# A second block table in two parts, and block and expert numbers loaded 18 and 21 at a time

## The reference

```python
x = x + xattn(layernorm(x), ctx, pos, pos, Wq, Wkv, Wout, bout)   # 32 heads of 8, axial rope, softmax
x = x + ffn(layernorm(x), Wg, W1, W2, W3)

def ffn(x, Wg, W1, W2, W3):                                       # 8 experts, hidden size 176
    scores = einsum('btd,ed->bte', x, Wg)
    topk_s, topk_i = top_k(scores, 2)
    probs = softmax(topk_s)
    onehot = topk_i[..., None] == arange(E)
    w = einsum('btk,btke->bte', probs, onehot)
    for e in range(E):
        h = silu(einsum('btd,hd->bth', x, W1[e])) * einsum('btd,hd->bth', x, W2[e])
        y = y + w[..., e:e+1] * einsum('bth,dh->btd', h, W3[e])
    return y
```

## Time and profile before

| | us |
|---|---|
| median of 3 runs (529.56 to 529.92) | 529.66 |
| the profiled execution | 529.24 |
| its span, first to last instruction | 527.3 |
| PE busy | 474.1 (90%) |
| DVE busy | 405.5 (77%) |
| POOL busy | 366.0 (69%) |
| ACT busy | 351.6 (67%) |

### The profile page before, as it was taken

How to read it: one execution, slowest core, us unless ns; L and a number is a source line. 1 busy time by engine, 2 the same in 40 slices (tenths; PEclk the granted TensorE clock), 3 DMA queues, 4 the chain that set the end, 5 groups by cost and what they waited for, 6 DMA issues and landing times.

```text
span 527.3 us, 21533 instructions
## 1 busy us (share of the span) xinstructions
PE 474.1 (90%) x7701; PEld 365.8 (69%) x7701; DVE 405.5 (77%) x1199; ACT 351.6 (67%) x929; POOL 366.0 (69%) x634
## 2 busy tenths in 40 slices
PE   3676899999999999999999999889899999899890
PEld 2563566676676766767666665559799999889780
DVE  7376689899898999999989898767655556776672
ACT  3473677877778777777777777667466666566550
POOL 4442758888888888888888887356666557675471
PEclk9787999999999999999999999899899999999895
DMA  6920101121121212212111110143654446877844
GB/s 192 235 71 7 30 20 54 40 74 43 60 66 49 94 52 70 65 48 67 40 61 56 50 35 25 44 120 96 195 158 132 127 127 202 251 236 240 303 146 159
DMA packets 43225, 54.55 MB, mean 103 GB/s; under 512 B 6727, under 2 KB 36849, under 8 KB 43122
## 3 DMA queue, kind: packets, MB, share of 16 engines
q1 hardware_dynamic: 36066, 35.79, 24.5%
q0 software_dynamic: 6480, 16.85, 8.9%
q10 hardware_dynamic: 576, 0.53, 0.3%
HBM read 29.60 MB, written 23.94 MB: 102 GB/s over the span
## 4 chain that ended last, share of the span: by engine, by line
PE 69%; DVE 12%; DMA 6%; issue 6%; SPq 2%; ACT 2%; POOL 2%; POOLq 0%; DVEq 0%; ACTq 0%
PE logit_banks L1551 9%; PE bank L1401 6%; PE logit_banks L1570 6%; PE logit_banks L1361 6%; PE logit_banks L1342 5%; PE bank L1388 5%; PE qkv_banks L1310 5%; PE logit_banks L1369 5%; PE bank L1394 4%; PE qkv_banks L1321 3%; DVE negmax L757 3%; PE qkv_banks L1301 3%; DMA y_in<-result_rows 3%; PE bank L1331 3%; PE bank L1539 2%
## 5 line engine op out<-in xcount | busy, mean ns | idle before, releaser
L691 POOL DMA_INDIRECT result_rows<-blocks_io,blk_dest x71 | 72.5, 1021 | 53.3 <-ACT blocks_io L1245 23.8
L657 POOL DMA_INDIRECT routed_rows<-xs,slots x64 | 65.7, 1026 | 16.7 <-issue 16.7
L757 DVE TENSOR_REDUCE negmax<-logit_banks 128x16 f32<-128x1024 f32 x64 | 75.0, 1212 | 2.3 <-PE logit_banks L1342 2.3
L1137 ACT ACTIVATE late<-logit_banks 128x1024 f32<-128x1024 f32 x64 | 62.0, 1021 | 14.4 <-PE logit_banks L1369 14.4
L664 POOL TENSOR_TENSOR ropes<-rope_a,ropes 128x512 f32<-128x512 f32 x32 | 41.2, 1288 | 29.5 <-DVE ropes L744 29.5
L1022 DVE TENSOR_TENSOR gated<-xn,logit_banks 128x176 f32<-128x176 f32 x71 | 23.8, 335 | 46.8 <-ACT xn L1251 45.8
L764 DVE RECIPROCAL rden<-bank 128x256 f32<-128x256 f32 x32 | 55.8, 1745 | 0.8 <-PE bank L1394 0.8
L648 POOL TENSOR_TENSOR mid<-mid,mask 128x512 f32<-128x512 f32 x44 | 44.7, 1035 | 11.8 <-ACT mid L1118 11.7
L1551 PE MATMUL logit_banks<-w_hi,x_hi 128*128 x142 | 47.0, 331 | 0.0
L1551 PE MATMUL logit_banks<-w_hi,x_lo 128*128 x142 | 46.4, 327 | 0.0
L1251 ACT ACTIVATE xn<-logit_banks 128x176 f32<-128x176 f32 x71 | 22.5, 316 | 35.7 <-PE logit_banks L1551 35.7
(11 more groups left out here) (219 smaller groups left out, 1378.8 us busy)
## 6 DMA issues: line engine op xcount, KB each, us to landing
blocks_io<-routed_rows SPq DMA_DIRECT2D x71, 129.0 KB, 2.4
y_in<-result_rows SPq DMA_DIRECT2D x16, 512.0 KB, 4.6
x_sb<-in_x_dram SPq DMA_DIRECT2D x32, 128.0 KB, 2.1
out_dram<-o_sb SPq DMA_DIRECT2D x16, 256.0 KB, 3.8
ctx_sb<-in_ctx_dram SPq DMA_DIRECT2D x32, 64.0 KB, 2.3
blocks_io<-in_L_ffn_W_dram SPq DMA_DIRECT2D x4, 512.0 KB, 6.8
mid<-mT SPq DMA_DIRECT2D x128, 4.0 KB
routed_rows<-pad_row SPq DMA_DIRECT2D x11, 129.0 KB, 2.9
```

The source lines that it names most:

```text
L657: nc.gpsimd.indirect_dma_start(routed[:, :], bass.IndirectOffsetOnAxis(ap=slots[:, t.slot(TR), k:k + 1], axis=0), xs[:, t.slot(TR), k, :], ...
L691: nc.gpsimd.indirect_dma_start(results[:, :], bass.IndirectOffsetOnAxis(ap=blk_dest[:, b.slot(RB):b.slot(RB) + 1], axis=0), y_sb[:, b.slot ...
L757: V.tensor_reduce(negmax[:, t.par, 16 * half:16 * half + 16], ps_s[:, 1024 * half:1024 * half + 1024].rearrange("p (h k) -> p h k", k=N), ...
L1137: S.activation(pT[:, 1024 * half:1024 * half + 1024], ps_s[:, 1024 * half:1024 * half + 1024], ACT.Exp, scale=SCALE).then_inc(exp_done, 1)
```

## The change

The second table is worked out twice by the same steps: once from the counts up to tile 28 (five groups) for blocks 17 to 48 (`MID` is 49), in the last two turns of DVE's attention pipeline and around the first two block splits, and once from all counts for blocks 49 to 70, in DVE's turns 14 to 17. SP copies the first of them behind block 7's load and the second behind block 27's. The padding DMAs of SP move from behind block 11's load to behind block 15's. Row numbers are loaded at blocks 0, 17, 35 and 53 (17, then 18 at a time), expert numbers at 0 (17), and during blocks 16, 34 and 52, 21 at a time from numbers 14, 32 and 50, into one set of registers.

```diff
-    T1, NG = GROUPS[0], len(GROUPS)
-    FULL = 2 * T1 - E + 1
+    T1, T2, NG = GROUPS[0], GROUPS[-2], len(GROUPS)
+    FULL, MID = 2 * T1 - E + 1, 2 * T2 - E + 1
...
-            row_starts, row_counts = chunks(RB)
-            row_regs = [sp.alloc_register(f"row{n}") for n in range(max(row_counts))]
+            row_starts = [0, FULL, 2 * FULL + 1, 3 * FULL + 2, NBLK]
+            row_regs = [sp.alloc_register(f"row{n}") for n in range(FULL + 1)]
...
                 if c == FULL:
-                    sp.wait_ge(rest_in, 32)
                     sp.wait_ge(pad_in, 16 * E)
...
                 if c in row_starts:
-                    load_rows(c, row_counts[row_starts.index(c)])
+                    if c == FULL:
+                        sp.wait_ge(mid_in, 32)
+                    if c == row_starts[2]:
+                        sp.wait_ge(rest_in, 32)
+                    load_rows(c, row_starts[row_starts.index(c) + 1] - c)
                 load_block(Turn(0, c, RB))
-                if c == RB + 3:
+                if c == RB - 1:
+                    sp.wait_ge(mid_done, 2)
+                    sp.dma_start(row_i[0:1, FULL:MID], rest_i[FULL:MID, 0:1]).then_inc(mid_in, 16)
+                    sp.dma_start(exp_i[0:1, FULL:MID], rest_i[FULL:MID, 1:2]).then_inc(mid_in, 16)
+                if c == FULL - 2:
                     for e, rows in enumerate(load_counts(sp, 0)):
                         pad_expert(sp, e, rows)
-                if c == FULL - 3:
+                if c == JOIN + 20:
                     sp.wait_ge(rest_done, 2)
-                    sp.dma_start(row_i[0:1, FULL:NBLK], rest_i[FULL:NBLK, 0:1]).then_inc(rest_in, 16)
-                    sp.dma_start(exp_i[0:1, FULL:NBLK], rest_i[FULL:NBLK, 1:2]).then_inc(rest_in, 16)
+                    sp.dma_start(row_i[0:1, MID:NBLK], rest_i[MID:NBLK, 0:1]).then_inc(rest_in, 16)
+                    sp.dma_start(exp_i[0:1, MID:NBLK], rest_i[MID:NBLK, 1:2]).then_inc(rest_in, 16)
...
                 full_blocks(t.c - T1 - 3)
+                if t.c >= T2 + 2:
+                    rest_blocks(t.c - T2 - 2, NG - 1, mid_done)
...
-            def rest_blocks(step):
+            def rest_blocks(step, ng, done):
...
-                rest_blocks(b.c - JOIN)
+                if b.c >= 2 * JOIN:
+                    rest_blocks(b.c - 2 * JOIN, NG, rest_done)
...
             scores(tile(T - 2))
+            rest_blocks(2, NG - 1, mid_done)
             split_xbT(Turn(0, 0, RB))
+            rest_blocks(3, NG - 1, mid_done)
             split_xbT(Turn(0, 1, RB))
...
-            exp_starts, exp_counts = chunks(4)
-            ahead = [[pe.alloc_register(f"expert{k}_{n}") for n in range(max(exp_counts))] for k in range(2)]
+            exp_starts = [FULL, 2 * FULL + 1, 3 * FULL + 2]
+            ahead = [pe.alloc_register(f"expert{n}") for n in range(FULL + 4)]
...
-                k = exp_starts.index(first)
-                if first == 0:
-                    pe.wait_ge(full_in, 32)
-                if first == FULL:
-                    pe.wait_ge(rest_in, 32)
-                regs = ahead[k % 2][:exp_counts[k]]
-                pe.load(regs, exp_i[0:1, first:first + exp_counts[k]])
+                count = min(FULL + 4, (FULL if first == 0 else NBLK) - first)
+                pe.wait_ge(*{0: (full_in, 32), FULL - 3: (mid_in, 32)}.get(first, (rest_in, 32)))
+                pe.load(ahead[:count], exp_i[0:1, first:first + count])
...
                 if b.c + 1 in exp_starts:
-                    load_experts(b.c + 1)
+                    load_experts(b.c - 2)
```

More of the change, by code:

```diff
@@ L326, in xattn_ffn_kernel @@
         gap_done, lean_done = sem("gap_done"), sem("lean_done")
-        full_in, rest_in = sem("full_in"), sem("rest_in")
+        full_in, mid_in, rest_in, mid_done = (sem(s) for s in ("full_in", "mid_in", "rest_in", "mid_done"))
         wg_done, wg_sb = sem("wg_done"), sem("wg_sb")
@@ L407, in blocks @@
                 body(do, Turn(0, c, RB))
-        def chunks(step):
-            starts = list(range(0, FULL - step // 2, step)) + list(range(FULL, NBLK, step))
-            return starts, [end - start for start, end in zip(starts, starts[1:] + [NBLK])]
         def group_of(v):
@@ L980, in full_blocks @@
                     V.tensor_scalar(full_i[:, 1:2], full_exp[:], float(E - 1), None, ALU.min).then_inc(full_done, 1)
-            def rest_blocks(step):
+            def rest_blocks(step, ng, done):
                 flat = "p g e -> p (g e)"
+                n = ng * E
                 if step == 0:
-                    whole(ups[:].rearrange(flat), cnts[:].rearrange(flat), UP)
+                    whole(ups[:, 0:ng].rearrange(flat), cnts[:, 0:ng].rearrange(flat), UP)
                     V.tensor_copy(prior[:, 0], full_cnt[:])
-                    tab(V.tensor_copy(prior[:, 1:NG], ups[:, 0:NG - 1]))
+                    tab(V.tensor_copy(prior[:, 1:ng], ups[:, 0:ng - 1]))
@@ L989, in rest_blocks @@
                 if step == 1:
[L990 to L994, removed]
@@ L995, in rest_blocks @@
-                    tab(V.tensor_tensor(seg_skip[:], seg_from[:, 1:NG * E + 1], seg_from[:, 0:NG * E], ALU.subtract))
+                    V.scalar_tensor_tensor(seg_from[:, 0:n], prior[:, 0:ng].rearrange(flat), float(P),
+                                           region_g[:, 0:ng].rearrange(flat), ALU.mult, ALU.add)
+                    V.memset(seg_from[:, n:n + 1], float(E * RC))
+                    tab(V.tensor_tensor(seg_cnt[:, 0:n], ups[:, 0:ng].rearrange(flat), prior[:, 0:ng].rearrange(flat),
+                                        ALU.subtract))
@@ L996, in rest_blocks @@
+                    tab(V.tensor_tensor_scan(seg_end[:, 0:n], ones_g[:, 0:n], seg_cnt[:, 0:n], float(FULL),
+                                             ALU.mult, ALU.add))
+                    tab(V.tensor_tensor(seg_skip[:, 0:n], seg_from[:, 1:n + 1], seg_from[:, 0:n], ALU.subtract))
                 if step == 2:
-                    tab(V.scalar_tensor_tensor(seg_skip[:], seg_cnt[:], -float(P), seg_skip[:], ALU.mult, ALU.add))
+                    tab(V.scalar_tensor_tensor(seg_skip[:, 0:n], seg_cnt[:, 0:n], -float(P), seg_skip[:, 0:n],
+                                               ALU.mult, ALU.add))
@@ L1001, in rest_blocks @@
                 if step == 3:
-                    tab(V.tensor_reduce(rest_row[:], seg_jump[:], AX_X, ALU.add))
+                    tab(V.tensor_reduce(rest_row[:], seg_jump[:, 0:n], AX_X, ALU.add))
                     tab(V.scalar_tensor_tensor(rest_row[:], jcol[:], float(P), rest_row[:], ALU.mult, ALU.add))
-                    V.tensor_tensor(rest_i[:, 0:1], rest_row[:], rest_base[:], ALU.add).then_inc(rest_done, 1)
-                    V.tensor_reduce(rest_exp[:], seg_past[:], AX_X, ALU.add)
@@ L1006, in rest_blocks @@
-                    tab(V.tensor_reduce(seg_over[:], seg_past[:].rearrange("p (g e) -> p g e", e=E)[:, :, E - 1], AX_X,
-                                        ALU.add))
+                    if ng == NG:
+                        dve.wait_ge(mid_in, 32)
+                    V.tensor_tensor(rest_i[:, 0:1], rest_row[:], rest_base[:], ALU.add).then_inc(done, 1)
+                    V.tensor_reduce(rest_exp[:], seg_past[:, 0:n], AX_X, ALU.add)
+                    tab(V.tensor_reduce(seg_over[:], seg_past[:, 0:n].rearrange("p (g e) -> p g e", e=E)[:, :, E - 1],
+                                        AX_X, ALU.add))
@@ L1510, in body @@
                     transpose_weights(range(6, 8))
-            exp_starts, exp_counts = chunks(4)
-            ahead = [[pe.alloc_register(f"expert{k}_{n}") for n in range(max(exp_counts))] for k in range(2)]
+            exp_starts = [FULL, 2 * FULL + 1, 3 * FULL + 2]
+            ahead = [pe.alloc_register(f"expert{n}") for n in range(FULL + 4)]
             experts = {}
             def load_experts(first):
-                k = exp_starts.index(first)
-                if first == 0:
-                    pe.wait_ge(full_in, 32)
-                if first == FULL:
-                    pe.wait_ge(rest_in, 32)
-                regs = ahead[k % 2][:exp_counts[k]]
-                pe.load(regs, exp_i[0:1, first:first + exp_counts[k]])
-                for n, reg in enumerate(regs):
+                count = min(FULL + 4, (FULL if first == 0 else NBLK) - first)
+                pe.wait_ge(*{0: (full_in, 32), FULL - 3: (mid_in, 32)}.get(first, (rest_in, 32)))
+                pe.load(ahead[:count], exp_i[0:1, first:first + count])
+                for n, reg in enumerate(ahead[:count]):
                     experts[first + n] = pe.snap(reg, min_val=0, max_val=E - 1)
```

6 lines of the change are left out of this document (3 added, 3 removed).

## The result

| | before | after |
|---|---|---|
| median of 4 runs on one chip, us | 529.79 (529.56 to 529.94) | 540.95 (538.87 to 544.39) |
| ratio to before | | 1.0217 [1.0159, 1.0275] |
| span of the profiled execution, us | 527.3 | 542.5 |
| PE busy, us | 474.1 | 479.5 |

The change costs 11.2 us. The forecast was 5.4 slower, 535.0; the direction holds, and of the cost less than half was foreseen. The ratios leave out runs over 1.5% above the fastest of their kernel (one each of e2_pe_fours, e4_aligned and e8_before_pads13), which the ranges show.

The account below looks back on a forecast made before the run. PE, 69% of the chain, was taken to bound the kernel, losing time to padding and register loads. Terms -3.9 - 9.3 + 13.8 + 3.3 + 1.2 + 0.3 = +5.4 gave 535.0 us, range 522 to 541.

Parts of the forecast that it names:

- Prices: Register loads: starts on multiples of four are read four at a time (0.28 a four), others at 0.235 us a number.
- the first 17: First loads of 17 numbers from 0, on PE and SP: +1.2 us in all.
- the three small loads ahead of 17: PE's loads ahead of number 17: 0.34 us each, hidden below the cover of PE's queue, costing nothing.
- The rival of cheap numbers: PE's three long loads: a number costs little however many are read, +4.7 us, total 522.5; chance 0.22.
- that of pairs: Loads from 14 and 50: even starts are read in pairs, three loads cost 9.0 us, total 530.3; chance 0.26.
- that of number by number everywhere: All register loads: numbers read singly whatever the start, 5.0 us for 32 as well, total 543.9; chance 0.08.
- Block 12's wait: Pads moved behind block 15's load: block 12's load no longer waits, -2.2 idle and -1.7 half clock, -3.9 us.
- the forecast's 9.3 for small loads: Fourteen PE loads from number 17 on removed: twelve at 0.38, one 1.12, one 1.98 plus 1.65 half clock; -9.3 us.
- Block 17: Block 17's load waits for pads and SP's 18 row numbers: PE stands 2.2, half clock 1.1, +3.3 us.
- the last one of the change part by part: SP's table copies and 18-row loads at 35 and 53: eight buffers of lead, nothing, or up to 2 us in the tail.
- a stall of 4.8 for each long load: PE's loads of 21 from 14 and 50: 4.8 us idle each plus 1.7 half clock; all three loads +13.8.

Follow-up runs that it names:

- e2_pe_fours: Changed kernel with PE's expert numbers loaded four at a time from 17, 21, ... as before; 535.91 us, ratio 1.0114.
- e4_aligned: Changed kernel with every long register load on PE and SP begun on a multiple of four, sizes about 20; 529.24 us, ratio 1.0000.
- e8_before_pads13: Kernel before with SP's four pad DMAs behind block 13's load instead of block 11's; 526.43 us, ratio 0.9980.
- e7_before_aligned: Kernel before with the second table stored three places further, so every four and eight begins on a multiple of four; 522.00 us, ratio 0.9872.
- e6_best: Changed kernel with small loads of fours and eights, all begun on multiples of four, and pads behind block 13's load; 518.83 us, ratio 0.9804.
- e1_prices: Kernel before with 13 more register loads of expert numbers at the end of PE's program, their numbers unused; 530.41 us in one run.
- e1b_prices: Kernel before with 13 more register loads at the end of PE's program, each followed by a matmul using its last number; 540.01 us in one run.
- e9_rows53_early: Changed kernel with SP's 18 row numbers from 53 loaded behind block 36's load into registers of their own; 541.80 us, ratio 1.0218.

## Why the prediction was wrong

**Prices: right.** 5.09 for 14 and 50 (5.0 forecast), 1.74 for 32 (1.7), 4.03 for SP's 18 from 17 (3.7), 1.54 for the first 17 (1.4 without the start). The start of a run decides, as the rows of before suggested, and e7_before_aligned and e6_best show the other side of it. Two readings of those rows were wrong without harm: the load of five from 12 took 0.79, so not all three small loads ahead of 17 last 0.34, below the cover, and the four from 0 cost 0.13 a number and not 0.09. The rival of cheap numbers and that of pairs were refuted by rows, that of number by number everywhere by the load from 32, though its time, 543.9, lay nearer to the result. The Trainium skill ("Runtime: NRT & Kernel Launch", section "Instruction fetch mechanics") has about 200 ns a register even in bulk, on a page that speaks of loads from HBM; the tables here lie in SBUF. These runs are near that figure for unaligned starts (0.24) and not for aligned ones (0.08 in four or eight).

**Gains: right, in part by luck.** Block 12's wait gave 3.67 of 3.9, the small loads of h18 to h50 and h55 to h70 gave 9.7, where the forecast had 8.6 there. But of the forecast's 9.3 for small loads, 3.6 came from one long one, the 2.59 from 65 with the half clock behind it. The same load lasted 1.69, 2.03 and 1.14 in e1_prices, e1b_prices and e8_before_pads13, and the stage was 1.9 to 3.2 shorter there, so part of this gain belongs to the one profile of before that both were read from.

**Block 17: right in kind, too small in size.** The pads' issue ended near 382.1, within 1 us of the forecast's 377.5 once 3.8 of the first stage and 1.6 of t28 to h0 are added. But the last of them landed 5.4 after it began (chain of after: the pad's DMA, SP's numbers, block 17's DMA):

```profile
381.78 5.43 DMA routed_rows<-pad_row
387.23 4.03 SPq L517
...
392.05 1.95 DMA blocks_io<-routed_rows
```

The forecast took the median landing of 2.9 for it. PE stood 3.96 instead of the 2.2 forecast. Part came back at once, since the load from 14 behind it stood only 3.50 of its forecast 4.8.

**The step that failed** is the last one of the change part by part: SP's 18 rows at 35 and 53 "have eight buffers of lead: nothing, or up to 2 in the tail". At 35 that held. At 53 it cost 4.80 of idle PE, with a stretch of 6.7 at the 1.2 GHz level that begins just before PE goes on. h50 to h55 took 6.1 more than forecast, as much as the whole miss: PE's idle there was 4.80 and 2.33 where 4.8 was forecast, and 10 us ran at half clock (476.1 to 482.8 and 486.3 to 489.6) where 3.4 were forecast. The lead was counted for the blocks' loads, and block 53's load was late for nobody. The `y_in` loads on the same queue have no such lead: they already landed late in before (DVE waited 1.2 for two of them), and SP's queue held one of them back for 4.5. The instruction moved was looked at with the thing it serves, not with what stands behind it on its queue. Reading the same numbers 17 blocks earlier took that wait away and 3.9 off the stage (e9_rows53_early). The other 2.2 stay with PE's load from 50, which lasted 6.38 there instead of the 5.0 forecast. This is shown in the stage; the time of the whole kernel did not fall with it.

**Stalls are not a sum.** The forecast added a stall of 4.8 for each long load to the wait at block 17. Alone, PE stood 5.0 to 5.7 for such a load; right behind another wait only 3.50 and 2.33 in after. The error here was on the side of too much, and hid part of the other.

## What to carry to other kernels

Lay a table in SBUF so that every register load begins on a multiple of four numbers (16 bytes here): that was worth 1.3% [0.5, 2.0] to a kernel with 18 small loads on PE and 9 on SP. The two groupings by about 20 gained nothing: no change where they began on multiples of four, 2.2% slower where they did not. A register load, a count or a wait put into a queue that also issues transfers can be paid by whatever stands next in that queue with the least lead, as `y_in` did here, so list those by kind before calling a step free. And read an experiment by its stages, where two stalls lie close, since taking one away can let the next stand in full.

## What the runs showed of the hardware that was not expected

Two numbers from 18 or 20 took 0.54 and 0.55 us, four from 20 took 0.34, one 0.31. Sixteen from 16 took 1.52, nearly as much as 21 from 20 (1.62), while eight took 0.6: the loads on multiples of four were not in proportion to their numbers. Identical instructions up to t0 took 63.5 to 67.4 us; the granted clock of before and after in the same early stretches (42.55 to 52.79 us: 0.67 and 0.50; 56.2 to 63.0: 1.00 and 0.50) shows where, not why. And idle time of nearly one length did not always bring the lower clock: behind the long loads on multiples of four (e4_aligned), PE stood 1.96, 1.82 and 1.84 us; the granted clock stayed at 1.00 behind the first two and was 0.50 from 479.5 to 482.8, behind the third.
